# All lower drives of a Mamba state loop turned by TensorE from diagonal matrices, and a quarter of the lower products with C moved to GpSimd

## The reference, cut to what matters

```
dt = softplus(...)                      # (B, L, 256)
A = -exp(Alog)                          # (256, 16)
def step(h, ins):
    dt_t, u_t, B_t, C_t = ins
    h = exp(dt_t[..., None] * A) * h + (dt_t * u_t)[..., None] * B_t[:, None, :]
    y_t = einsum('bdn,bn->bd', h, C_t)
    return h, y_t
```

## Time and profile before

| what | us |
|---|---|
| median of 3 executions | 854.9 |
| the profiled execution, its own time | 857.5 |
| its span (first to last instruction) | 855.7 |
| TensorE, VectorE, ScalarE, GpSimd busy | 696.7, 586.6, 592.3, 416.2 |
| first scan of the state loop begins | 114.97 |
| stages in order, cut where ScalarE copies dtuT for the next | 55, 54.6, 54.7, 54.6, 55.9, 62.9, 60.3, 49.5 |

### The profile page before, as it was taken

The page is one execution under the profiler, slowest core; times in us unless marked ns, Lnnn a source line. Parts: engine busy times, 40 slices in busy tenths (PEclk is TensorE's granted clock), DMA queues, the critical chain, the costliest instruction groups (busy, mean ns, idle before and its releaser), DMA issues.

```text
span 855.7 us, 13132 instructions
## 1 busy us (share of the span) xinstructions
PE 696.7 (81%) x4243; PEld 483.0 (56%) x4243; DVE 586.6 (69%) x851; ACT 592.3 (69%) x1220; POOL 416.2 (49%) x362
## 2 busy tenths in 40 slices
PE   6899976887877978879769766588897898889886
PEld 4588845565665655746647546577682333334433
DVE  6335689997988979879778778984425445554542
ACT  3255468888988788878797886955526666765663
POOL 6110167897987978969768877940000000000000
PEclk8889988799897998978869978989998999999998
DMA  3224545565563544636535439500300000000000
GB/s 108 99 54 140 167 131 151 142 183 144 151 189 125 169 146 142 191 105 174 154 117 154 149 102 273 189 1 1 98 1 1 1 1 1 1 1 1 13 13 26
DMA packets 48131, 85.80 MB, mean 100 GB/s; under 512 B 6320, under 2 KB 11448, under 8 KB 48064
## 3 DMA queue, kind: packets, MB, share of 16 engines
q1 hardware_dynamic: 48064, 84.96, 33.0%
HBM read 83.37 MB, written 1.57 MB: 99 GB/s over the span
## 4 chain that ended last, share of the span: by engine, by line
PE 44%; ACT 24%; issue 15%; DVE 14%; POOL 2%; DVEq 0%; DMA 0%; POOLq 0%; ACTq 0%
ACT scaled L794 5%; ACT ps L778 5%; PE ps L1659 5%; PE ps L1710 3%; PE ps L1951 3%; PE ps L1725 3%; PE ps L1597 3%; ACT decay_sb L778 3%; DVE moe L1091 2%; PE ps L1920 2%; PE ps L1639 2%; DVE ps L1091 2%; PE ps L1928 2%; DVE hc L1099 2%; PE ps L1601 2%
## 5 line engine op out<-in xcount | busy, mean ns | idle before, releaser
L584 POOL TENSOR_TENSOR drive<-dtu,b_sb 128x512 f32<-128x512 f32 x160 | 203.8, 1281 | 1.1 <-DMA b_sb<-bc_rows 0.4
L592 POOL TENSOR_TENSOR hc<-moe,c_sb 128x512 f32<-128x512 f32 x128 | 163.4, 1277 | 47.3 <-DVE moe L1091 47.1
L1091 DVE TENSOR_TENSOR_SCAN moe<-ps,drive 128x512 f32<-128x512 f32 x128 | 153.4, 1199 | 0.0
L1659 PEld LDWEIGHTS ps<-ident,hc 128*128 128x128 f32 x1024 | 133.0, 156 | 32.5 <-issue 26.3
L1659 PE MATMUL ps<-ident,hc 128*128 128x128 f32 x1024 | 150.2, 299 | 0.0
L998 ACT ACTIVATE probs<-ps 128x1024 f32<-128x1024 f32 (+1 forms) x96 | 87.9, 916 | 79.0 <-PE ps L1928 68.0
L1091 DVE TENSOR_TENSOR_SCAN ps<-decay_sb,ps 128x512 f32<-128x512 f32 x96 | 117.4, 1223 | 35.4 <-PE ps L1639 20.4
L1639 PE MATMUL ps<-ident,scaled 128*128 128x128 f32 x384 | 67.0, 302 | 71.0 <-ACT scaled L794 63.5
L794 ACT ACTIVATE scaled<-dtuT,bT 128x128 f32<-128x128 f32 x384 | 121.4, 388 | 0.0
L778 ACT ACTIVATE ps<-dt,negA 128x510 f32<-128x510 f32 x160 | 105.9, 676 | 2.7 <-DVE ps L1103 1.7
L597 POOL TENSOR_TENSOR stat<-stat,halfc 128x4 f32<-128x4 f32 x7 | 7.0, 1006 | 204.2 <-DVE stat L1319 204.2
(11 more groups left out here) (264 smaller groups left out, 1210.4 us busy)
## 6 DMA issues: line engine op xcount, KB each, us to landing
b_sb<-bc_rows SPq DMA_DIRECT2D x128, 256.0 KB, 3.3
c_sb<-bc_rows SPq DMA_DIRECT2D x128, 256.0 KB, 3.4
wbuf<-in_pack SPq DMA_DIRECT2D x16, 514.0 KB, 3.3
wbuf<-in_pack SPq DMA_DIRECT2D x8, 512.0 KB, 4.1
x_sb<-in_x SPq DMA_DIRECT2D x4, 256.0 KB, 3.5
out<-x_sb SPq DMA_DIRECT2D x4, 256.0 KB, 2.3
w_in<-in_w_in SPq DMA_DIRECT2D x1, 512.0 KB
bc_rows<-bcx SPq DMA_DIRECT2D x8, 64.0 KB, 2.9
```

The source lines that it names most:

```text
L584: pool.tensor_tensor(drive_of(N, half), dtu[:, N // STATES % 2, half], b_sb[:, N % B_RING], ALU.mult) \
L592: pool.tensor_tensor(hc[:, 2 * (N % DEEP) + half], h_of(q), c_sb[:, N % C_RING], ALU.mult).then_inc(sem["hc_pooled"], 1)
L1091: dve.tensor_tensor_scan(h_of(q)[:, turn], decay_bank(q)[:, turn], source[:, turn], 0.0, ALU.mult, ALU.add).then_inc(sem["scan_done"], 1)
L1659: last = pe.matmul(ps[:, Y_BANK + half, block], hc[:, 2 * (N % DEEP) + half, block], ident[:], start=False, stop=True, is_transpose=True, ...
```

## The change

1. Every lower drive is now made by TensorE: `turn_drive(N)` runs for all N and is a plain f32 matmul of `dtuT` (stationary) with a diagonal matrix of B (`spots`) in place of a transpose of a scaled copy. ScalarE's `scale_drive`, `bT` and the events "b" are gone.
2. The diagonal matrices are built in DRAM. Four areas `spot_rows` are filled with zeros once. For each state SyncE stores the 512 values of B onto the diagonals of four 128x128 blocks (`store_spots`, single elements, DRAM to DRAM) and one round later loads the area as a tile of 128x512 (`load_spots`), into a ring of three that takes the place of three quarters of `xm`.
3. For every fourth state (`lent(N)`: N % 4 == 3) the lower scan writes to SBUF (`h_lent`), and GpSimd multiplies it with C. GpSimd's drives are the upper half's alone.
4. Decay buffers: upper states use the three PSUM banks, lower ones the two SBUF tiles. TensorE turns drives 0 and 1 in state 0.

```diff
+def lent(N):
+
+    return N % 4 == 3
...
+        spot_rows = nc.dram_tensor("spot_rows", (SPOT_ROWS, P, COLS), F32).ap()
+
+        def spot_places(k):
+
+            return bass.AP(spot_rows.tensor, k * P * COLS, [[COLS + 1, P], [P, 4]])
...
         def h_of(q):
             N, half = divmod(q, HALVES)
-            return h[:, N % 2] if half else ps[:, H_BANKS[N % OWN_H]]
+            return h[:, N % 2] if half else h_lent[:] if lent(N) else turned_bank(N)
...
+            sp.wait_ge(sem["zero_tile"], 1)
+            for k in range(SPOT_ROWS):
+                sp.dma_start(spot_rows[k], c_sb[:, C_RING - 1]).then_inc(sem["zero_stored"], 16)
...
+            def store_spots(N):
+
+                n = N
+                if n == 0:
+                    sp.wait_ge(sem["zero_stored"], 16 * SPOT_ROWS)
+                if n >= SPOT_ROWS:
+                    before = n - SPOT_ROWS
+                    sp.wait_ge(sem[f"spots_loaded{before % SPOT_RING}"], 16 * (before // SPOT_RING + 1))
+                sp.dma_start(spot_places(n % SPOT_ROWS), bc_rows[N // STATES, N % STATES].rearrange("(t p) -> p t", p=P),
+                             allow_slow_non_contiguous=True) \
+                    .then_inc(sem[f"spots_stored{n % SPOT_ROWS}"], 16)
+
+            def load_spots(N):
+
+                n = N
+                if n == 0:
+                    sp.wait_ge(sem["ln_copied"], STAGE["T"]["T", 1, PAIRS - 1] + 1)
+                after(sp, "drive_turned", n - SPOT_RING + 1)
+                sp.wait_ge(sem[f"spots_stored{n % SPOT_ROWS}"], 16 * (n // SPOT_ROWS + 1))
+                sp.dma_start(spots[:, n % SPOT_RING], spot_rows[n % SPOT_ROWS]).then_inc(sem[f"spots_loaded{n % SPOT_RING}"], 16)
...
                 load_b(N)
                 load_c(N)
+                store_spots(N)
+                if N:
+                    load_spots(N - 1)
...
                     if N:
+                        if lent(N - 1):
+                            times_c(N - 1, 0)
                         times_c(N - 1, 1)
                     if M < ALL:
-                        drive_half(M, 1)
+                        drive_upper(M)
...
-                if N + 1 < ALL and turned(N + 1):
-                    scale_drive(N + 1)
-
-            def scale_drive(N):
-
-                g, j, n = N // STATES, N % STATES, turned_before(N)
-                if n == 0:
-                    act.wait_ge(sem["e0_down"], PAIRS0)
-                act.wait_ge(sem["side_free"], SIDE["t", g] + 1)
-                act.wait_ge(sem["side_free"], SIDE["b", g] + 1)
-                after(act, "drive_turned", n - 1)
-                for t in range(4):
-                    block = slice(t * P, (t + 1) * P)
-                    last = act.activation(scaled[:, n % 2, block], dtuT[:, block], ACT.Copy, scale=bT[:, t, j:j + 1])
-                last.then_inc(sem["drive_scaled"], 1)
...
-                times_c(N)
+                if not lent(N):
+                    times_c(N)
...
             def turn_drive(N):
 
-                n = turned_before(N)
-                pe.wait_ge(sem["drive_scaled"], n + 1)
-                after(pe, "hc_ready", N - OWN_H + 1)
+                n = N
+                pe.wait_ge(sem[f"spots_loaded{n % SPOT_RING}"], 16 * (n // SPOT_RING + 1))
+                pe.wait_ge(sem["side_free"], SIDE["t", N // STATES] + 1)
+                before = N - OWN_H
+                if before >= 0 and lent(before):
+                    pe.wait_ge(sem["scan_done"], HALVES * before + 1)
+                elif before >= 0:
+                    pe.wait_ge(sem["hc_ready"], own_before(HALVES * before) + 1)
                 if N == 1:
                     pe.wait_ge(sem["side_free"], SIDE["dt", 0, 1] + 1)
                 for t in range(4):
                     block = slice(t * P, (t + 1) * P)
-                    last = pe.transpose(ps[:, H_BANKS[N % OWN_H], block], scaled[:, n % 2, block], ident[:])
+                    last = pe.matmul(ps[:, H_BANKS[N % OWN_H], block], dtuT[:, block], spots[:, n % SPOT_RING, block], start=True, stop=True)
                 last.then_inc(sem["drive_turned"], 1)
...
-                    if ev[1] + 1 < ALL and turned(ev[1] + 1):
+                    if ev[1] == 0:
+                        turn_drive(0)
+                    if ev[1] + 1 < ALL:
                         turn_drive(ev[1] + 1)
```

More of the change, by code:

```diff
@@ L252, with lent_before, own_before, pooled_drive @@
 PREP = {ev: n for n, ev in enumerate(ev for ev in FILL + AT_ORDER if ev[0] in ("T", "L", "Q", "K", "O1", "O2"))}
+def lent(N):
+    return N % 4 == 3
+def lent_before(N):
+    return N // 4
 def shared_before(q):
-    return q // HALVES
[L260 to L282, removed]
+    N, half = divmod(q, HALVES)
+    return N + lent_before(N) + (half and lent(N))
+def own_before(q):
+    N, half = divmod(q, HALVES)
+    return N - lent_before(N) + (half and not lent(N))
+def pooled_drive(q):
+    return q % HALVES == 1
+def drives_before(q):
+    return q // HALVES
 POOLED = [q for q in range(HALVES * ALL) if pooled_drive(q)]
@@ L374, in build @@
         e0.close()
-        drive = sb("drive", [P, DRIVES + 2, COLS])
+        drive = sb("drive", [P, DRIVES, COLS])
+        h_lent = sb("h_lent", [P, COLS])
         decay_sb = sb("decay_sb", [P, SB_DECAYS, COLS])
-        scaled = sb("scaled", [P, 2, COLS])
+        spots = xm[:].rearrange("p t d -> p (t d)")[:, COLS:4 * COLS].rearrange("p (n c) -> p n c", n=SPOT_RING)
         h = moe[:].rearrange("p t d -> p (t d)")[:, 0:2 * COLS].rearrange("p (n c) -> p n c", n=2)
@@ L542, in _ @@
         def _(pool):
+            pool.memset(c_sb[:, C_RING - 1], 0.0).then_inc(sem["zero_tile"], 1)
             pool.memset(halfc[:], -0.5).then_inc(sem["halfconst"], 1)
@@ L638, in _ @@
                         pool.wait_ge(sem["dtu_ready"], HALVES)
+                        pool.wait_ge(sem["e0_down"], PAIRS0)
                         for first in range(DRIVES - 1):
-                            for half in range(HALVES):
-                                if half or first and not turned(first):
-                                    drive_half(first, half)
+                            drive_upper(first)
                     M = N + DRIVES - 1
@@ L657, in _ @@
                     pool.wait_ge(sem["u_ready"], g + 1)
[L658 removed]
+                    after(pool, "drive_ready", STATES * (g - 1))
                     if g > 1:
@@ L1578, in project @@
                                          start=False, stop=(k == TAPS - 1))
-                elif kind == "b":
-                    pe.wait_ge(sem["side_free"], SIDE["x", g] + 1)
-                    for t in range(4):
-                        last = pe.transpose(side[:, t * STATES:(t + 1) * STATES], bcx[0:STATES, t * P:(t + 1) * P], ident[0:STATES, 0:STATES])
                 elif kind == "t":
```

71 lines of the change are left out of this document (33 added, 38 removed).

## The result

The changed kernel takes 901.25 us (median of 4 runs, 898.47 to 903.03) against 855.61 us (median of 4, 852.6 to 859.49) for the kernel before on the same chip: ratio 1.0495, 95% interval 1.0458 to 1.0533. It is slower by 45.6 us, outside the predicted range of 836 to 880. The profiled execution has a span of 895.7 us, 40.0 more than before.

What follows compares the result with a forecast made beforehand. VectorE was taken to set the pace, with ScalarE making it late. Terms 5 + 3 x 0.4 - 0.9 - 6.2 - 3.6 - 0.3 = -4.8 us on the profiled 857.5 gave a median of 851 to 852, range 836 to 880.

Steps and rivals of the forecast that it cites:

- the part on transfers: SyncE's queue: waiting for each store's landing before loading costs nothing up to 7 us; last stage loses 3 us (0 to 12).
- The time of the DMA engines: Ordinary stage: 16 more loads at 0.95 us each make 45.8 of 55 us busy; each store adds 0.4 (0 to 0.87).
- Rival D: Single-element stores cost over 18 ns an element; at 27 ns a stage needs 59.9 us of DMA, total 886; chance 0.11.
- an ordinary stage: State loop: terms for scans, D, projections, moved products and small waits sum to +0.4 us a stage, giving 55.0.
- The norm stages: Two stages with norms on ScalarE: without scaled copies 56.7 us against 62.9 and 60.3, so -6.2 and -3.6.
- rival B: TensorE stays at 2.4 GHz, so x takes 1.70 us: -1.6 in seven stages, 841 us; chance 0.26.
- Rival C: Low clock of a stage's last third persists into states 0 to 3: about +15 us, 866; chance 0.22.
- State 4: Its scan, behind D, add_y and the turn, starts 6.36 us after state 3's instead of 4.02: +2.3 us.
- The first scan: Loop start: drives of states 0 and 1 stand behind half-clock projections, moving it from 114.97 to about 119.2, +4.2 us.
- The first stage: Start of the state loop: the later first scan and half a unit to one more cost +5 us.
- The last stage: Stage of 49.5 us: products save 2.3, norms' stalls 2, state 4's turn costs 1, transfers 3; together -0.3 us.
- The moved products: Four products a stage go from VectorE to GpSimd; those of states 11 and 15 save 1.2 us a stage.

## Why the prediction was wrong

**The step that failed** is in the part on transfers: "It waits for a store's landing before it loads, one round (some 3 us) after its issue", and then "no cost, up to a landing of 7 us". I set the landing against the lead that one load has before its reader (7.6 us for spots, 10 for b and c). That is right for a single late transfer and wrong for a wait that recurs in an in-order queue: it limits the rate. With one round between issue and wait, a round can't be shorter than half of landing and issues, so the bound was 2 x 3.4 - 1.3 = 5.5 us, and it landed after 5.9. The kernel with early stores shows what this is worth: 38.6 us. A second wait of the same kind, for the landing of B and C at each stage's start, was not in the forecast either; it was there before, when SyncE had time to spare (it stood 221.2 us waiting for GpSimd's products between 110 and 620 us).

**The landing itself** I did not bound, though the earlier trace rows and the page's 256 KB loads were there to start from. It is 3.7 to 4.4 us where only the stores run or where only a part of the states has both, and 5.5 to 5.9 where loads and single elements run for every state. This gives the rest: loads 3.7 us alone, stores 0, together 23.3. I had put both at 3, in the last stage only; in its first form the last stage alone lost 16.3.

**The time of the DMA engines** was nearly right in sum, by two errors: a store 0.76 us where I took 0.4 (bounds 0 to 0.87), a load 0.77 where I took 0.95. Together 1.53 a state against 1.35. Rival D asked for more than 18 ns an element and the rows give 24, so its condition came true and its sign, TensorE waiting for spots in ordinary stages, too. But its reason, a stage that needs more DMA time than it has, did not: with 0.82 x 64.1 = 52.6 us of it in the 55 I forecast, the work fits. The order of one queue did the larger part (38.6 us) and loads and single elements together the rest (23.3). A chance of 0.11 for anything over 880 was too low, because I had let one mechanism stand for all that transfers could do.

**The engines' part can be read in the kernel with neither stores nor loads**, the same instructions without the transfers. Busy time of two ordinary stages, the two with norms, and the last:

```profile
170.06:224.41 54.35, 48.72 (x342) 39.72 (x341) 46.52 (x50) 32.11 (x51) 47.12 (x40) 0.97 0.49 157
224.41:278.90 54.49, 48.86 (x342) 39.75 (x341) 46.52 (x50) 32.13 (x51) 47.12 (x40) 0.97 0.55 157
388.00:445.60 57.60, 49.61 (x346) 40.23 (x345) 48.57 (x53) 36.96 (x73) 50.20 (x44) 0.97 0.53 154
445.60:501.60 56.00, 49.00 (x346) 40.90 (x344) 47.57 (x50) 36.88 (x72) 49.66 (x43) 0.98 0.50 156
...
501.60:552.80 51.20, 40.51 (x326) 38.65 (x326) 45.31 (x49) 28.98 (x69) 47.41 (x42) 0.93 0.63 196
```

Point by point: an ordinary stage was to be 55.0 us and is 54.3 to 54.6. The norm stages were to be 56.7 and are 57.6 and 56.0. ScalarE was to be near 31 and is 32.1. TensorE was to be at 50 or more; it is 48.7 here, since the clock is granted at 0.97 where it was 0.91 in the earlier trace rows (a part of rival B), though the x projection is still slow, 2.89 us for three of its instructions at 260.29. Rival C's spreading low clock is nowhere in these stages. State 4 came out as worked out. It is the state whose scan waits for D, add_y and the turn. Same kernel, in order of time:

```profile
237.88 1.22 DVE L1103 TENSOR_TENSOR_SCAN h_lent<-decay_sb,ps 128x512 f32<-128x512 f32 x1
...
240.34 2.05 PE L1666 MATMUL ps<-diagD,u_s 128*128 128x128 f32 x16 [0.84 <-DVE yg L1140]
242.23 1.04 PE L1675 MATMUL ps<-ident,hc 128*128 128x128 f32 x8
243.10 1.06 PE L1652 MATMUL ps<-xm,dtuT 128*128 128x128 f32 x8
...
244.26 1.23 DVE L1103 TENSOR_TENSOR_SCAN ps<-decay_sb,ps 128x512 f32<-128x512 f32 x1 [2.85 <-PE ps L1652]
```

From scan to scan 6.38 us against 6.36 forecast, D to add_y 1.89, add_y to turn 0.87, the turn 0.89 from start to next start, and "nearly 3 us" of wait is 2.85. The first scan, in the changed kernel, was to come near 119.2:

```profile
119.77 1.23 DVE L1107 TENSOR_TENSOR_SCAN ps<-decay_sb,ps 128x512 f32<-128x512 f32 x1 [6.10 <-PE ps L1657]
```

**Mis-sized terms of the engines' part.** This kernel is 17.6 us under before in span, where my sum without the transfers' 3 us was 7.8. Two terms make 7.8 of these 9.8 us. The first stage: I added 5 us for the late first scan, but in this kernel the stage's end stands at 170.06 against 170.50 before, although its first scan is at 121.06; it is made up within the stage, and no run isolates how. The last stage with what follows it: 52.4 + 289.8 us before, 51.2 + 285.3 here, -5.7 where I had -3.3 without transfers. The moved products, -1.2 us a stage on paper, gave 2.5 us in all, inside the uncertainty: VectorE has 46.5 us of work in 54.4, so what is taken off it can fall into its waits for TensorE and ScalarE (argued, not measured). In the ordinary stages this miss is hidden by others of the opposite sign: 54.4 instead of 55.0. The sum of the terms there was also added wrongly: they give +0.25 us a stage and not +0.4, some 1 us over all stages, which changes nothing in the account.

**The scale of the errors**: engines 10 us too pessimistic, transfers 59 too optimistic (62.0 measured between the changed kernel and the one with neither, 3 forecast).

## What to carry to other kernels

A wait that recurs once per round in an in-order issuing queue is priced as a rate, not as a lead: the round can't be shorter than (landing + issues between the wait's end and the next issue) / (rounds in flight), and that is compared with the round the engines need. Take the landing at the DMA load of the kernel after, not of the one before, and move such an issue one round earlier before judging the rest of a change. Look for every such wait in the queue, those at a stage's start too. A scheme that replaces engine work by transfers can be tried for a fraction of the iterations first; here half was the best.

## What the runs showed of the hardware

A DRAM to DRAM store of 512 single elements took 24 ns of an engine's time for each, about that of a 512 B piece loaded in the earlier trace rows (27 ns): the small pieces saved almost nothing of it. A landing grew with the share of the DMA engines well before they were full: 3.2 us at a share of 0.5, 4.1 to 4.5 at 0.71 to 0.79, 4.9 at 0.79 to 0.88 in the changed kernel and 5.3 at 0.83 to 0.93 with early stores, for the same 256 KB load of b. And an f32 matmul of the 128x128 drive, two instructions, took 1.06 us for its eight instructions against 0.60 for a transposed drive's four in the earlier trace rows, as the earlier trace rows had let expect.
